# An attention and mixture-of-experts kernel: rotation spread over the expert slots, keys stored once, results stored by ScalarE's queue

## The reference

```python
xn = layernorm(x)                                   # x: [2, 1024, 256]
# attention: 16 query heads, 4 key heads, head size 16
Q, K, V = heads(xn @ W_q), heads(xn @ W_k), heads(xn @ W_v)
Qr, Kr = rope(Q), rope(tile(K, 4))
attn = softmax(Qr @ Kr.T / 4) @ tile(V, 4) @ W_o
# experts: 8, two chosen for each token
top2, chosen = top_k(xn @ Wr, 2);  p = softmax(top2)
for e in range(8):
    w_e = sum(p where chosen == e)
    g = clip(silu(xn @ Wg[e]), -7, 7)
    ffn += ((g * (xn @ Wu[e])) @ Wd[e]) * w_e
return x + attn + ffn
```

## Time and profile before

| | us |
|---|---|
| median of 3 runs | 579.81 (579.05 to 579.84) |
| profiled execution, device time | 576.07 |
| its span | 574.3 |
| start, to the first gate product of slot 0 | 59.6 |
| slots, to the first gate product of slot 38 | 164.7 |
| the rest (tail of the slots, attention, end) | 350.0 |

### The profile page before, as it was taken

One profiled execution on the slowest core, in us unless ns is written; L12 is line 12 of the kernel. 1 busy time (PEld: TensorE's weight loads), 2 busy tenths in 40 slices (PEclk: granted clock), 3 DMA queues, 4 the chain that ended last, 5 costly groups with the idle time before them and its releaser, 6 DMA issues.

```text
span 574.3 us, 9921 instructions
## 1 busy us (share of the span) xinstructions
PE 526.5 (92%) x3464; PEld 249.3 (43%) x3464; DVE 396.3 (69%) x920; ACT 383.5 (67%) x548; POOL 173.2 (30%) x208
## 2 busy tenths in 40 slices
PE   1996748897999998999999999999999999999997
PEld 1832324454555554444444444444444444444433
DVE  4578756961666666587788887888888788785123
ACT  3421412431333433799999999999999999998673
POOL 3015854541222210012416422551344342600000
PEclk9997987897999999999999999999999999999999
DMA  8950235566642120310511421422224113100101
GB/s 293 375 184 1 80 133 170 169 183 193 170 138 74 59 62 29 103 38 19 131 47 45 115 58 41 102 65 75 57 58 119 31 57 84 30 2 21 46 29 55
DMA packets 39566, 53.72 MB, mean 94 GB/s; under 512 B 7936, under 2 KB 25728, under 8 KB 39520
## 3 DMA queue, kind: packets, MB, share of 16 engines
q1 hardware_dynamic: 32624, 40.25, 23.9%
q0 software_dynamic: 3408, 9.31, 5.9%
q10 hardware_dynamic: 3488, 3.55, 1.8%
HBM read 36.18 MB, written 16.65 MB: 92 GB/s over the span
## 4 chain that ended last, share of the span: by engine, by line
PE 73%; DVE 12%; DMA 6%; issue 3%; ACT 2%; SPq 2%; POOL 2%; DVEq 0%; ACTq 0%; POOLq 0%
PE bank L1249 21%; PE bank L1239 9%; PE bank L1112 9%; PE bank L1167 8%; PE bank L1129 7%; PE bank L1235 6%; PE bank L1184 4%; PE bank L1285 3%; DMA k_st<-rope_low 3%; PE bank L1122 2%; DMA rows_out<-xn 2%; DVE xn_t L907 2%; DVE xn L983 2%; SPq L378 1%; PE bank L1072 1%
## 5 line engine op out<-in xcount | busy, mean ns | idle before, releaser
L702 ACT ACTIVATE big<-bank 128x1024 f32<-128x1024 f32 x256 | 252.9, 1024 | 18.6 <-PE bank L1239 18.3
L1249 PE MATMUL bank<-big,v_st 128*32 128x256 f32 (+1 forms) x1472 | 148.3, 474 | 2.8 <-DVE xn L983 2.8
L1239 PE MATMUL bank<-qs,kb 64*128 64x512 f32 x512 | 120.0, 408 | 0.7 <-ACT big L702 0.7
L904 DVE TENSOR_REDUCE mx<-bank 128x1 f32<-128x512 f32 x128 | 87.8, 686 | 27.9 <-PE bank L1129 20.1
L899 DVE TENSOR_REDUCE mx<-bank 128x1 f32<-128x512 f32 x128 | 87.9, 687 | 22.1 <-PE bank L1114 20.0
L1167 PE MATMUL bank<-big,xn 128*128 x156 | 82.6, 654 | 15.9 <-ACT xn L671 15.4
L907 DVE CUSTOM_DVE_ANT_0 xn_t<-bank,xn_t 128x512 f32<-128x512 f32 x128 | 87.5, 684 | 4.5 <-PE bank L1129 1.5
L657 ACT ACTIVATE xn_t<-bank 128x512 f32<-128x512 f32 x128 | 76.7, 599 | 20.4 <-PE bank L1114 12.2
L1239 PEld LDWEIGHTS bank<-qs,kb 64*128 64x128 f32 x512 | 57.7, 185 | 19.4 <-ACT big L702 12.3
L1112 PE MATMUL bank<-ka,qs 64*128 64x512 f32 x128 | 63.4, 495 | 0.4 <-DVE mx L904 0.4
L1114 PE MATMUL bank<-ka,qs 64*128 64x512 f32 x128 | 63.3, 495 | 0.0
(11 more groups left out here) (140 smaller groups left out, 611.7 us busy)
## 6 DMA issues: line engine op xcount, KB each, us to landing
qs<-q_hl SPq DMA_DIRECT2D x64, 128.0 KB, 2.7
rows_out<-xn SPq DMA_DIRECT2D x39, 128.0 KB, 2.6
ka<-k_st SPq DMA_DIRECT2D x16, 256.0 KB
kb<-k_st SPq DMA_DIRECT2D x16, 256.0 KB
xs<-in_L_attn_x SPq DMA_DIRECT2D x4, 512.0 KB, 6.3
big<-in_L_ffn_Wg SPq DMA_DIRECT2D x16, 128.0 KB, 6.5
big<-in_L_ffn_Wu SPq DMA_DIRECT2D x16, 128.0 KB, 6.6
big<-in_L_ffn_Wd SPq DMA_DIRECT2D x16, 128.0 KB, 6.5
```

Of the source, the lines that this page charges most:

```text
L702: act.activation(probs[kt % 2][:, 2 * j:2 * j + 2, :].rearrange("p r q -> p (r q)"), st_ps[j][:, :], ACT.Exp, scale=1.0 / math.sqrt(HD)).t ...
L904: nc.vector.reduce_max(mx[h][:, STEPS + k, 1:2], max_bank(v, i), axis=X_AXIS).then_inc(mx_taken, 1)
L1239: last = mm(out[i], kb[p][half[i], kt // QT, keys], qs[q][half[i], j, :], start=False, stop=True, skip_group_check=kt % 2 == 1)
L1249: last = mm(o_ps[32 * r:32 * (r + 1), columns], v_st[p][:, key_block(kt), :], probs[kt % 2][:, r, columns], start=(kt == 0 and columns.sta ...
```

## The change

- The 12 parts come in another order (keys of batch 0, queries of batch 0, then batch 1) and are done at slots 1, 3, 5, 7, 9, 11, 14, 17, 20, 23, 26, 29; there are four sets of buffers. The last block's projections are copied by ScalarE at slot 2.
- A key part is stored by two transfers instead of four, to `k_hl`, where a row stands once; each load of `ka` or `kb` is 8 transfers whose source is read twice (`twice`), instead of 2.
- Results are stored by ScalarE's queue (the last two by SP).
- `SHARED` is 26 instead of 21. Scores start from the maxima at every fourth key tile instead of every second; `values_between` is used at three of four key tiles and splits the values 128 and 384 instead of 256 and 256.
- The counting chain uses two scans; GpSimd's half of `in_tile` moves to VectorE; the count is asked for ahead of the first keys' projection, and all of block 3's projections go behind the inversion.
- 24 products of `ident` with itself at TensorE's start; the router weights are padded to 128 columns.

```diff
-            return sum(32 if PARTS[o][1] < 2 else 64 for o in range(q % 3, q, 3))
+            return 32 * len(range(q % NB, q, NB))
+        PART_SLOTS = (1, 3, 5, 7, 9, 11, 14, 17, 20, 23, 26, 29)
+        KEYS_LOAD, FIRST_LOAD, SECOND_LOAD = 6, 10, 14
+        LATE_LOADS = {18: (0,), 21: (1,), 24: (2, 3), 27: (4, 5)}
-        SHARED = 21
+        SHARED = 26
...
-                    for j, half in enumerate((rope_hi, rope_hi, rope_lo, rope_lo)):
-                        sp.dma_start(k_st[b, :, HD * j:HD * (j + 1), k % 2, :],
-                                     half[n][0:KV * HD, :].bitcast(F32)).then_inc(done, 16)
+                    k_rows = [k_hl[b, k % 2, j].rearrange("d (u c) -> u d c", u=2) for j in range(2)]
+                    sp.dma_start(k_rows[0], rope_hi[n][:, :].bitcast(F32)).then_inc(done, 16)
+                    sp.dma_start(k_rows[1], rope_lo[n].bitcast(F32)).then_inc(done, 16)
...
+            def twice(g, j, half, cols):
+                kv = g % KV
+                return k_hl[g // KV, half, j, HD * kv:HD * (kv + 1), cols].unsqueeze(0).to_broadcast(
+                    [2, HD, cols.stop - cols.start])
             def load_ka(g, p):
-                src = k_st[g // KV, g % KV]
-                sp.dma_start(ka[p][0:STACK, :, :].bitcast(F32), src[:, :, QUART:KCOLS]).then_inc(ka_loaded[p], 16)
-                sp.dma_start(ka[p][STACK:P, :, :].bitcast(F32), src[:, :, 0:HALF]).then_inc(ka_loaded[p], 16)
+                for half in range(2):
+                    for j in range(2):
+                        low, high = 2 * HD * j, STACK + 2 * HD * j
+                        sp.dma_start(ka[p][low:low + 2 * HD, half, :].bitcast(F32),
+                                     twice(g, j, half, slice(QUART, KCOLS))).then_inc(ka_loaded[p], 16)
+                        sp.dma_start(ka[p][high:high + 2 * HD, half, :].bitcast(F32),
+                                     twice(g, j, half, slice(0, HALF))).then_inc(ka_loaded[p], 16)
...
+            def parts_stored(last):
+                for q in range(max(0, last - NB + 1), last + 1):
+                    sp.wait_ge(qk_stored[q % NB], stored_before(q + NB))
+
+            for t in range(SLOTS):
+                q = part_at(t)
+                if q is not None:
+                    store_part(q)
+                if t == KEYS_LOAD:
+                    parts_stored(1)
+                    load_ka(0, 0)
+                if t == FIRST_LOAD:
+                    parts_stored(3)
+                    load_q(0, 0, 0)
+                if t == SECOND_LOAD:
+                    parts_stored(5)
+                    load_q(0, 1, 1)
...
-                if kt % 2 == 0:
+                if kt % QT == 0:
                     for i in parts:
                         mm(out[i], ones_r[half[i], :], ms[v][half[i], j, :], start=True, stop=False)
...
+            for _ in range(24):
+                mm(idle_ps, ident[:, :], ident[:, :], start=True, stop=True)
```

More of the change, by code:

```diff
@@ L125, in build @@
         n_tiles = sb("n_tiles", [P, E])
-        cum = [sb(f"cum{i}", [P, E]) for i in range(2)]
+        ends = sb("ends", [P, E])
+        starts = sb("starts", [P, E])
+        slot_row = sb("slot_row", [P, SLOTS])
         slot_no = sb("slot_no", [P, SLOTS, E])
@@ L236, in build @@
         lo_ready = sem("lo_ready")
-        qk_stored = [sem(f"qk_stored{m}") for m in range(3)]
+        qk_stored = [sem(f"qk_stored{m}") for m in range(NB)]
         route = sem("route")
@@ L368, in store_part @@
                 k, m = PARTS[q]
[L369 removed]
+                n, done = q % NB, qk_stored[q % NB]
                 b, cols = k // 2, slice(k % 2 * HALF, (k % 2 + 1) * HALF)
@@ L422, in load_m @@
                                  m_turned[i][32 * n:32 * (n + 1), :]).then_inc(m_loaded[i], 16)
-            for m in range(3):
-                sp.wait_ge(qk_stored[m], stored_before(NP + m))
-            for t in range(NP, SLOTS):
+            def parts_stored(last):
[14 more added lines that the diff above has]
+                    load_q(0, 1, 1)
+                for n in LATE_LOADS.get(t, ()):
+                    sp.wait_ge(rows_t_ready, t)
+                    if n == 0:
+                        load_kb(0, 0)
+                    elif n == 1:
+                        load_ka(1, 1)
+                    else:
+                        load_q(1, (n - 2) // 2, 2 + (n - 2) // 2, [n % 2])
                 if t == SLOTS - 7:
@@ L430, in _ @@
                     load_m(0)
[L431 to L442, removed]
+            for t in range(SLOTS - 2, SLOTS):
+                sp.wait_ge(y_copied, t + 1)
+                sp.dma_start(rows_out[bass.ts(t, P), :], y_s[t % 4]).then_inc(y_stored[t % 4], 16)
+            parts_stored(NP - 1)
             def period(g, p, last):
@@ L641, in _ @@
                     act.activation(projected(k, m)[0:rows_m, :], pj_ps[k][m][0:rows_m, :], ACT.Copy).then_inc(pj_copied, 1)
+            for k in range(BLOCKS - 1):
+                copy_projected(k)
             act.wait_ge(hot_tile_ready, 1)
@@ L681, in _, with store_y @@
                            ACT.Copy).then_inc(rows_t_ready, 1)
-            for q in range(AHEAD - 1):
-                high_part(q)
-            for t in range(NP):
-                expert(t, t % 2, first=t == 0)
-                if t + AHEAD - 1 < NP:
-                    high_part(t + AHEAD - 1)
-            for t in range(NP, SLOTS):
-                expert(t, t % 2, last=t == SLOTS - 1, beside=shared_with(t))
+            def store_y(t, i):
+                act.wait_ge(y_copied, t + 1)
+                act.dma_start(rows_out[bass.ts(t, P), :], y_s[i]).then_inc(y_stored[i], 16)
+            for t in range(SLOTS):
+                expert(t, t % 2, first=t == 0, last=t == SLOTS - 1, beside=shared_with(t))
+                if t == 0:
+                    high_part(0)
+                if t == 2:
+                    copy_projected(BLOCKS - 1)
+                if t >= 3:
+                    store_y(t - 3, (t - 3) % 4)
+                if part_at(t) is not None and part_at(t) + AHEAD - 1 < NP:
+                    high_part(part_at(t) + AHEAD - 1)
+            store_y(SLOTS - 3, (SLOTS - 3) % 4)
             act.wait_ge(ht_ready, SLOTS)
@@ L808, in _ @@
[L808 to L810 removed]
+            link(nc.vector.tensor_tensor_scan(ends[:, :], ones[:, 0:E], n_tiles[:, :], 0.0, ALU.mult, ALU.add))
+            link(nc.vector.tensor_scalar(starts[:, 1:], ends[:, 0:E - 1], float(P), None, ALU.mult))
```

255 lines of the change are left out of this document (117 added, 138 removed).

## The result

The changed kernel takes 622.51 us (median, 622.12 to 624.36), the kernel before 579.74 beside it: ratio 1.0747, 95% interval 1.0723 to 1.077. The prediction was 618. The profiled span is 620.3 us against 574.3, so 46.0 longer; the forecast span was 612.

A forecast was written before the change was run, and what follows sets the result against it. TensorE, 73% of the chain, was taken as the bound, waiting for slow transfers in the slots. Start and slots -5, loads in attention +47 and products -4 gave +38 on 579.8: 618 us, 8 in 10 within 552 to 658.

The forecast's parts named there:

- start: Before slot 0: inverting products run earlier, less what block 3's projections behind the inversion cost; -3.6 us (0 to -6).
- slots without transfers: Slots 0 to 38, transfer waits left out: 134.3 us instead of 164.7, plus 4 for late VectorE parts; -26.4 us.
- waits in the slots: Slow key transfers hold up slot 9 by 5 us and slot 13 by 18.7, plus 1.5 for half clock; +25.2 us.
- loads in attention: Groups 0 to 5: `ms` lands 6.4 us late behind key loads, plus 1.5 for half clock; 6 x 7.9 = +47 us.
- products: Attention: three of four key tiles at 2.46 us instead of two, four restarts fewer at the end; -4 us (0 to -6).
- Two engines by the outermost count of either side: Key stores and loads: the smaller outermost count of both sides, 2, confines a transfer to 2 engines; chance 0.70.
- 557: Rival: key loads go by the side they write, all engines, only stores on two; 557 us, chance 0.11.
- 546: Rival: no key store or load is confined to two engines, the change's gain comes in whole; 546 us, chance 0.12.
- the one of 584: Rival: two engines at their best, 24 GB/s, `ms` 3.4 us late; 584 us (576 to 592), chance 0.07.
- The rate: Attention key loads: 22 GB/s taken for each of two engines, between 15.7 and 24; 1.05 MB in 23.8 us.
- Costed at nothing: Start: identity products that warm TensorE and the padded router weights change nothing (-1 to +1 us).
- carrying 5.5 us of difference: Whole kernel: the median stood 5.5 us above the profiled span of 574.3, and this was kept for the forecast.

The follow-up runs named there:

- e11: The kernel of e3 with the first queries' load at slot 8 instead of 10: 544.01 us, 0.9452 of the kernel before the change.
- e3: Changed kernel with key loads as transfers of 16 rows of both halves and key stores as four transfers of 64 rows: 548.80 us, 0.9529 of the kernel before.
- e5: The same program as e3, run again as yardstick for later runs: 545.87 us, 0.9492 of the kernel before the change.
- e1: Changed kernel with each key load taking 16 rows of both halves, no repeated source, stores unchanged: 558.85 us, 0.9699 of the kernel before.
- e2: Changed kernel with key parts stored by four transfers of 64 rows, loads unchanged: 607.56 us, 1.0567 of the kernel before.
- e12: The kernel of e3 with SP issuing the maxima's transfers ahead of the next group's keys: 545.14 us, 0.9474 of the kernel before.
- e8: The kernel of e3 with the twelve rotation parts in slots 0 to 11, one after another: 570.16 us, 0.9904 of the kernel before.
- e7: The kernel of e3 with the attention products as before the change: 549.98 us, 0.9542 of the kernel before.
- e9: The kernel of e5 without the 24 identity products, router weights still padded to 128 columns: 548.09 us, 0.953 of the kernel before.
- e4: Changed kernel with SP issuing the maxima ahead of the keys, loads and stores still on two engines: 563.9 us, 0.9788 of the kernel before.
- e10: The kernel of e5 with 72 columns of router weights, the 24 identity products kept: 551.44 us, 0.9571 of the kernel before.

## Why the prediction was right, step by step

The sum by the marks of slot 0, slot 38 and the end, span against span, one profiled execution of each:

| term | predicted | measured | from |
|---|---|---|---|
| start | -3.6 | -2.7 | 56.89 against 59.59 |
| slots without transfers | -26.4 | -24.8 | e11, 139.9 against 164.7 |
| waits in the slots | +25.2 | +20.0 | 159.9 against 139.9 |
| loads in attention | +47 | +58.2 | 403.6 against 345.4 (e3, e5 and e11 alike) |
| products | -4 | -4.6 | 345.4 against 350.0 |
| sum | +38 | +46.1 | 620.3 against 574.3 |

- *Two engines by the outermost count of either side.* Shown for the loads as they stand, the repeated source included. The share is 0.13 as named, and e1, which changes only the shape of the loads, takes back 63.6 us of span. The rule of the Trainium skill cited ahead is now borne out by a broadcast source too, with 52 GB/s at 0.13. The rivals of 557 and 546 fall by that share; the one of 584 by the `ms` waits, 6.07 us each and not 3.4.
- *Loads in attention*, the term that was mis-sized. Its waits are right: 25.2 us from first issue to landing against 25.8, and 36.4 / 6 = 6.07 against 6.4. What was too small is the price beside the wait: 1.5 us in the prediction, (58.2 - 36.4) / 6 = 3.6 in this execution. I took it from one gate product, but in group 0 half clock holds to 253.7, 3.2 us behind the wait and over more than a key tile, and in group 2 to 356.1, 6.2 us behind it. By the marks of `ms` products, which stand four key tiles apart, the 3.6 can be placed. The four tiles behind a wait took 12.2 to 13.5 us where e3 has 10.4: 2.7 a group. The first four tiles of the next group took 10.6 to 12.1 where e3 has 10.4: 0.6, partly in waits for ScalarE. The remaining 0.3 stands in the four tiles with the wait. The price is not fixed: in e2 it was 2.0.
- *The rate*, too low: 26 GB/s for an engine, not 22, and above the 24 that I gave as the upper end. The landing came out right because two errors met, which is luck. Packets flow from 227.8, 2.5 us behind the first issue, 1.05 MB at 52 GB/s take 20.2, and the last 2.5 go to the two engines' part of `ms` and `qs` and to landing, where I had 23.8 and 2. That SP's issues stretched from 0.57 to 1.17 us did not hold the packets up: from 229 to 243 the DMA share is 0.14 at 53 GB/s, never below 0.13, so the two engines always had work.
- *Waits in the slots.* Part 1 landed at 96.9 (94 predicted), `high_part(5)` waited 5.63 us (5) and held up slot 11, not slot 9, slot 13 waited 12.3 for its queries (18.7), which landed at 119.4 (121). The wait was smaller mostly because the slots ahead of it came later: slot 12 began at 103.97, where I had slot 13 due at 102.3. The stores are the larger part: from slot 0 to 38 e2, without slow stores, takes 148.4 us and e1, without slow loads, 154.7.
- *Slots without transfers.* Right to 2 us, which is also as near as single executions tell: e3, e5 and e12 took 142.2, 144.5 and 143.5 with a queries' wait of 2.3 to 2.5. e8 shows that nearly all of it is the spread: parts in a row cost 24 us. The 3 us on VectorE for a part was right, 2.9 in e5 and 3.2 in e8.
- *Products.* The sum is right and its working is not: the share of the groups was half of the -4, and they gave 1. e7 accounts for 2.7 of the 4.6. The other 1.9 lies between the kernel before and e7, in small pieces over groups 1 to 6; what makes it stays open.
- *Costed at nothing.* The identity products are: e9. The padding isn't, in this kernel: 3 to 6 us of medians, the clock in the start. Against the profiled execution of the kernel before it shows no gain, 26.05 against 26.00 for the first queries. The start itself varies: slot 0 stood between 55.0 and 57.7 in the eleven traces with 128 columns, so the 0.9 between -3.6 and -2.7 says nothing.
- The median is 42.8 us longer where the span is 46.0; carrying 5.5 us of difference between the two over to the changed kernel was too much, there it is 2.2. Without that the forecast would have been 3 us lower.
- *Near by luck.* 618 against 622.5 is nearer than the terms were: the loads were 11.2 us too small, the waits in the slots 5.2 and the carried difference 3.3 too large.

The loss is thus no loss of the idea. Its start, slots and products give 2.7 + 24.8 + 4.6 = 32.1 us, and transfers with 2 leading steps took 78.2 away again (20.0 and 58.2; some 2 to 5 of the 20.0 stand in e3 and e5 too, which have all transfers on more engines and a queries' wait that e11 lacks). e11, without them and with its queries early, has the lowest median here, 0.9452 of the kernel before.

## What to carry to other kernels

Before a store or load is reshaped to save bytes or copies, read the outermost count on both of its sides. With the smaller of the two, if it is under 16, estimate the time as bytes / (count x rate of one engine), here 24 to 26 GB/s for counts of 4 and 2. Then ask which small, urgent transfer stands behind it on the same queue; if the shape can't be helped, moving that transfer ahead can give back all of it (e4). And count a wait of 6 or 7 us as 9 to 10 (9.7 in the changed kernel, 8.8 in e2): the half clock behind it is part of its price.

## What the runs showed of the hardware

- A transfer confined to two engines moves 52 GB/s, 26 an engine, while all 16 together gave 246, 15.7 an engine.
- Issuing is not free of the transfer's shape: eight 64 KB loads took SP 5.02 us with two engines and 3.59 with sixteen; single ones went from 0.57 to 1.17 us once many were under way, and one store of queries behind the key stores took 4.80 (at 83.98) where others take 0.58.
- Half clock behind a wait of 6 us held for 3.2 us in group 0 and for 6.2 in group 2, behind the wait that ended at 349.9, with no idle time of TensorE in between:

```profile
351.00:356.00 5.00, 5.00 (x27) 1.82 (x26) 2.92 (x9) 2.91 (x4) 0.00 (x1) 0.50 0.00 0
```

- The width of the router products moved the first queries by 3.3 us (e10 with 72 columns, e9 with 128) at an unchanged arrival of the rows. With 72 the clock stayed at 0.50 to 26 us in e10, but not in the kernel before, which has 72 too.
